# A mixture-of-experts stage that stores its results in token order with indirect scatters, and the stage behind it that reads them with plain loads

## The chip, the core and the metric

The kernel runs on one core of one Trainium2 chip. The metric is the device time of one execution in microseconds (us). The engines are TensorE (PE; its weight loads are listed apart as PEld), VectorE (DVE), ScalarE (ACT), GpSimd (POOL) and SyncE (SP), which issues DMAs. Each runs its own program in order, and they wait for each other on semaphores.

## The reference

16384 tokens (128 sequences of 128) of width 128, all in float32. Two layers, each with a retention and a feed-forward part; every part takes the normalised h and adds to it:

```python
h = tok_ref(x)                                   # three-tap embedding
h = h + attn0(layernorm(h))                      # retention, 8 heads
gate = softmax(xn @ gate_w + gate_b)             # xn = layernorm(h)
top_v, top_i = top_k(gate, 2); top_w = softmax(top_v)
for e in range(8):                               # experts, 128 -> 512 -> 128
    ce = sum(where(top_i == e, top_w, 0), -1)
    out += ce[..., None] * (relu(xn @ w1[e] + b1[e]) @ w2[e] + b2[e])
h = h + out
h = h + attn1(layernorm(h))                      # retention with complex weights
h = h + merged_ffn(layernorm(h))                 # weights mixed per sequence
```

The experts are computed sparsely: each token goes through its two experts only.

## The kernel before, in words

The program has four stages, one after the other: retention with routing (tiles `a_...`), experts (`b_...`), complex retention (`c_...`) and the merged feed-forward layer (`d_...`). h stays in SBUF (`h_all`). Stages a and c work in 32 groups of 4 sequences (GB = 4, 512 tokens). Each engine has one list of pieces for a step, written out by hand, in which piece k works on group n + k; the steps in the middle run in a loop, two groups in one turn, and the first and last ones are unrolled.

**Stage a.** POOL gathers embedding rows (4 indirect DMAs per group, L330). Later in the group, DVE finds each token's two experts (`choose`, L860 and L864) and its place in each expert's list (`place_tokens`, to `pos_cur`). POOL copies these places to `pos_all` (L339) and scatters the normalised rows `xn_mid` to the DRAM tensor `sent` in 8 indirect DMAs of 128 rows (L343), 4 of them at the end of one step and 4 at the beginning of the next. PE's products there begin with L399 (from the gathered rows) and L410 (the transposes of the normalised rows). At the end DVE works out the table of slots (L988 to L1042), and with it `moves`, by which a place in `sent` becomes a place in `done`.

**Stage b** goes through 78 slots: 57 of 512 rows and 21 of 256. A slot is a run of rows of one expert. The first 76 slots are 19 laps of three large and one small one (ROUND = 4), and 17 of the laps are a loop. SP loads the rows (`b_x`, L1155), the two weights (`b_w`, L1161 and L1164) and the bias (`b_b`, L1167), two slots ahead; the load of the fourth slot waits for fills with zeros, which POOL writes behind the lists (L1173 to L1180). PE multiplies (L1232, four banks), transposes the next slot's rows (L1223) and multiplies back (L1242). ACT and DVE take the ReLUs in turns (L1262, L1288). DVE adds the bias of the slot before (`y_keep`, L1296) and POOL stores it in the order of the slots with one plain DMA (L1208). In the first four slots POOL also turns `pos_all` into places in `done` (`move_places`, L1196 to L1204).

**Stage c.** POOL gathers each group's two result rows per token from `done` (8 indirect DMAs, L1462, two groups ahead), DVE adds them to h (L1805, L1812) and takes the statistics, ACT normalises, PE transposes (L1516) and goes through the products of a group: L1531 (queries), L1554 (states, small matmuls from `k_early`), L1570 (scores), L1591 and L1597 (values), L1609 (back to the tokens), L1620, L1630. DVE masks the scores (L1841) and the states (L1849), ACT copies the queries (L1709). POOL also makes `k_early` and `q_late` (L1473, L1480). SP has only the load of constants (L1440), and then of `tv` for stage d (L1443), which waits for the first group's h.

Of the kernel before, what the change touches and what calls it, by code (L numbers as in the profile page):

```python
# [7 lines left out]
ALU = mybir.AluOpType  # L8
# [10 lines left out]
GB = 4  # L19
# [11 lines left out]
PACK = B2 + D  # L31
# [9 lines left out]
SPARE_ROWS = SMALL_SPARE * TILE  # L41
SEQS = 16
# [77 lines left out]
def retention_phase(nc, h_all, w_all, pos_all, routing, sent_d, ids_d, table_d, wq_d, wqs_d, wkkv_d,  # L120
                    gn_w_d, gn_b_d, tabs_d, tabs_c_d, gate_w_d, gate_c_d, slot_c_d):
# [12 lines left out]
    with ExitStack() as ctx:  # L134
# [40 lines left out]
        slots, list_end, moves, _ = routing  # L175
# [13 lines left out]
        xn_mid = sb("xn_mid", [P, 2, GB, D])  # L189
# [33 lines left out]
        shifts = sb("shifts", [P, 2, E])  # L223
# [7 lines left out]
        ids_padded = sem("ids_padded")  # L231
# [53 lines left out]
        pos_kept = sem("pos_kept")  # L285
# [5 lines left out]
        LOADS = 11  # L291
# [7 lines left out]
        def _(sp):  # L299
# [11 lines left out]
            sp.dma_start(routing[3][:], tabs_c_d[:, 2 * P:3 * P]).then_inc(loaded, 16)  # L311

        @block.gpsimd
        def _(pool):
# [57 lines left out]
            pool.memset(ids[:, NB:], 0).then_inc(ids_padded, 1)  # L372
            pool.wait_ge(ids_loaded, 16)
            pool.wait_ge(ids_padded, 1)
# [4 lines left out]
            pool.wait_ge(pos_kept, NG)  # L379

        @block.tensor
        def _(pe):
# [128 lines left out]
            def turn_mid(s, g):  # L511
# [5 lines left out]
                for b in range(GB):  # L517
                    m = nc.tensor.transpose(work[1][:, b * T:(b + 1) * T], xn_mid[:, g.par, b, :], ident)
# [76 lines left out]
        def _(act):  # L595
# [33 lines left out]
            def mid_normalise(g):  # L629
# [4 lines left out]
                for b in range(GB):  # L634
                    m = nc.scalar.activation(xn_mid[:, g.par, b, :], h_all[:, bass.ds(g.n * GB + b, 1), :],
                                             ACT.Identity, scale=rstd_mid[:, b:b + 1], bias=shift_mid[:, b:b + 1])
# [93 lines left out]
        def _(dve):  # L730
# [125 lines left out]
            def choose(g):  # L856
# [5 lines left out]
                m.then_inc(chosen_step, 1)  # L862
                dve.wait_ge(chosen_step, g.n * 2 + 1)
# [17 lines left out]
            def place_tokens(g):  # L881
# [5 lines left out]
                if g.is_past(2):  # L887
                    dve.wait_ge(pos_kept, g.n - 1)
# [93 lines left out]
            def then(ins):  # L982
# [40 lines left out]
            base = region[:, 0, :]  # L1023
            also(v.tensor_copy(moves[:, 0, 0, :], base))
            also(v.scalar_tensor_tensor(out=moves[:, 1, 0, :], in0=used[:, 0:E], scalar=float(TILE), in1=base,
                                        op0=ALU.mult, op1=ALU.add))
            also(v.scalar_tensor_tensor(out=shifts[:, 0, :], in0=ends[:, 0:E], scalar=float(TILE), in1=base,
                                        op0=ALU.mult, op1=ALU.subtract))
            then(v.tensor_scalar(shifts[:, 1, :], reached[:, 0:E], float(SMALL), float(BIG * TILE), ALU.mult, ALU.add))
            then(v.tensor_tensor(shifts[:, 1, :], shifts[:, 1, :], moves[:, 1, 0, :], ALU.subtract))  # L1030
            also(v.tensor_tensor(moves[:, 1, 1, :], shifts[:, 1, :], shifts[:, 0, :], ALU.subtract))
            also(v.tensor_copy(moves[:, 0, 1, 0:1], shifts[:, 0, 0:1]))
            also(v.tensor_tensor(moves[:, 0, 1, 1:E], shifts[:, 0, 1:E], shifts[:, 1, 0:E - 1], ALU.subtract))
# [11 lines left out]
def experts_phase(nc, pos_all, routing, sent_d, done_d, pack_d):  # L1045


    slots, list_end, moves, ident = routing

    with ExitStack() as ctx:  # L1050
# [11 lines left out]
        zeros = sb("zeros", [P, J, D])  # L1062
        pos_f = sb("pos_f", [P, 2, NB, 2])
        moved = sb("moved", [P, NB, 2])
        x = sb("x", [P, 2, J, D])
        w = sb("w", [P, 2, B2])
        b2 = sb("b2", [P, 2, D])
# [4 lines left out]
        zeroed = sem("zeroed")  # L1072
# [1932 lines left out]
```

## Time and profile before

| | |
|---|---|
| time, median of 3 runs | 2535.09 us (2529.93 to 2538.09) |
| profiled execution: span | 2547.7 us; its own time is not given apart from the span |
| PE busy | 2127.2 us (83%) |
| DVE, ACT, POOL busy | 1437.5, 1346.8, 1044.3 us |
| DMA | 168.12 MB, mean 66 GB/s |
| mean granted clock of PE | 0.893 |

Views of the profile used here: the table of stretches gives busy time, number of instructions, granted clock (1.00 is 2.4 GHz, 0.50 is 1.2 GHz) and the share of the DMA engines' time. The list of waits says which engine and line stood idle, and what ended it: "issue" is idle time in which the engine waited for nothing that the profile shows, "remote" a releaser that it cannot name. The timeline merges equal instructions and puts idle time before them in brackets.

### The profile page before, as it was taken

How to read it: one execution, taken by the hardware profiler on the slowest of the kernel's cores; microseconds unless marked ns; L12 is line 12 of the kernel's file. 1: busy time of each engine (PE TensorE's matmuls, PEld its weight loads, DVE VectorE, ACT ScalarE, POOL GpSimd, SP SyncE). 2: the span in 40 equal slices, each digit the busy share in tenths (PEclk: the TensorE clock that was granted, in tenths of full speed). 3: DMA queues.
4: the chain of work that ended last, by engine and by line, in shares of the span. 5: the costliest groups of instructions: out<-in, count | busy, mean ns of one | idle time of the engine just before them, and what ended most of it. 6: DMA issues, size and time to landing. Idle time of an engine off the chain costs nothing. (4 is left out here: it accounts for less than half of the span.)

```text
span 2547.7 us, 56802 instructions
## 1 busy us (share of the span) xinstructions
PE 2127.2 (83%) x19420; PEld 1576.5 (62%) x19420; DVE 1437.5 (56%) x4270; ACT 1346.8 (53%) x2844; POOL 1044.3 (41%) x1133
## 2 busy tenths in 40 slices
PE   5888888888875999999994777777777779999998
PEld 2555555555554677777772455554455558999997
DVE  3766666666664222222323455554555567888877
ACT  3655555555552222222223555555555568999985
POOL 3556656656645600000005444444444402334444
PEclk8989989988985999999996788877888789999999
DMA  2111211211211555555551210000000001111111
GB/s 71 53 57 50 59 57 49 59 57 49 59 32 34 181 163 158 165 158 168 152 166 51 102 26 22 23 22 25 25 23 23 21 5 35 39 35 38 48 39 43
DMA packets 101867, 168.12 MB, mean 66 GB/s; under 512 B 19714, under 2 KB 50699, under 8 KB 101620
## 3 DMA queue, kind: packets, MB, share of 16 engines
q1 hardware_dynamic: 70900, 87.99, 12.1%
q0 software_dynamic: 30848, 78.56, 10.3%
q8 instruction: 73, 1.20, 0.2%
q14 instruction: 46, 0.38, 0.0%
HBM read 121.45 MB, written 45.02 MB: 65 GB/s over the span
## 5 line engine op out<-in xcount | busy, mean ns | idle before, releaser
L1288 DVE TENSOR_SCALAR b_hT<-b_hbank,b_w 128x512 f32<-128x512 f32 (+1 forms) x156 | 105.8, 678 | 369.8 <-PE b_hbank L1232 369.7
L343 POOL DMA_INDIRECT sent<-a_xn_mid,a_pos_cur x256 | 250.5, 979 | 73.4 <-issue 72.8
L1462 POOL DMA_INDIRECT c_rows<-done,c_cur_pos x256 | 244.3, 954 | 75.1 <-issue 74.7
L1262 ACT ACTIVATE b_hT<-b_hbank,b_w 128x512 f32<-128x512 f32 (+1 forms) x156 | 98.3, 630 | 322.7 <-PE b_hbank L1232 322.7
L1242 PE MATMUL b_bank<-b_w,b_hT 128*128 128x128 f32 x2160 | 254.2, 275 | 2.1 <-DVE b_hT L1288 2.1
L1242 PEld LDWEIGHTS b_bank<-b_w,b_hT 128*128 128x128 f32 x2160 | 247.5, 192 | 2.4 <-DVE b_hT L1288 2.3
L1232 PE MATMUL b_hbank<-b_xT,b_w 128*128 128x512 f32 (+1 forms) x624 | 247.1, 539 | 0.9 <-DMA b_w<-pack_dram 0.9
L1841 DVE TENSOR_TENSOR c_masked<-c_bank,c_decay 128x512 f32<-128x512 f32 x256 | 163.3, 681 | 138.3 <-remote 102.0
L1208 POOL DMA_DIRECT2D done<-b_y x78 | 42.3, 543 | 423.4 <-DVE b_y L1296 405.3
L450 PE MATMUL a_bank<-a_wkkv,a_xT 128*128 128x384 f32 x256 | 120.8, 557 | 106.3 <-issue 94.6
L744 DVE TENSOR_TENSOR a_masked<-a_scores,a_tabs 128x1024 f32<-128x1024 f32 x128 | 155.3, 1221 | 45.3 <-PE a_scores L474 25.3
L607 ACT ACTIVATE a_kv<-a_bank 128x384 f32<-128x384 f32 x128 | 62.4, 488 | 208.9 <-PE a_bank L450 112.9
L1232 PEld LDWEIGHTS b_hbank<-b_xT,b_w 128*128 128x128 f32 x624 | 113.4, 192 | 87.8 <-issue 83.2
L1473 POOL TENSOR_TENSOR c_k_early<-c_xn,c_k_decay 64x512 f32<-64x512 f32 x32 | 40.9, 1277 | 299.9 <-ACT c_xn L1683 299.8
L2536 ACT ACTIVATE d_wm<-d_bank 128x448 f32<-128x448 f32 (+1 forms) x160 | 147.3, 1095 | 26.0 <-PE d_bank L2262 25.6
L1591 PE MATMUL c_bank<-c_masked,c_vx 128*32 128x128 f32 x2048 | 119.8, 337 | 44.6 <-issue 43.2
L2715 DVE COPY d_wm<-d_bank 128x448 f32<-128x448 f32 (+1 forms) x160 | 144.5, 1055 | 21.3 <-PE d_bank L2262 21.3
L1554 PE MATMUL c_bank<-c_xn,c_k_early 64*32 64x32 f32 x1024 | 53.5, 204 | 118.6 <-issue 111.2
L2262 PE MATMUL d_bank<-d_g_diag,tv 64*128 64x112 f32 (+1 forms) x2368 | 144.7, 277 | 6.9 <-ACT d_wm L2536 5.1
L2262 PEld LDWEIGHTS d_bank<-d_g_diag,tv 64*128 64x128 f32 x2368 | 137.9, 190 | 13.0 <-ACT d_wm L2536 6.4
L450 PEld LDWEIGHTS a_bank<-a_wkkv,a_xT 128*128 128x128 f32 x256 | 41.4, 201 | 160.8 <-issue 160.5
L330 POOL DMA_INDIRECT a_rows<-table_dram,a_cur_ids x128 | 125.5, 980 | 34.6 <-issue 34.6
(256 smaller groups left out, 4925.9 us busy)
## 6 DMA issues: line engine op xcount, KB each, us to landing
b_w<-pack_dram SPq DMA_DIRECT2D x78, 258.0 KB, 2.7
b_w<-pack_dram SPq DMA_DIRECT2D x78, 256.0 KB, 2.7
b_x<-sent SPq DMA_DIRECT2D x57, 256.0 KB, 2.7
done<-b_y POOLq DMA_DIRECT2D x57, 256.0 KB, 2.4
d_b_all<-b_rows SPq DMA_DIRECT2D x32, 256.0 KB, 3.4
out_dram<-h_all SPq DMA_DIRECT2D x32, 256.0 KB, 2.3
b_b<-pack_dram SPq DMA_DIRECT2D x78, 64.0 KB, 1.9
tv<-tv_dram SPq DMA_DIRECT2D x1, 4736.0 KB, 15.7
```

Source lines behind the costliest of these rows:

```text
L330: pool.indirect_dma_start(out=rows[:, p, b, :], out_offset=None, in_=table_d, in_offset=bass.IndirectOffsetOnAxis(ap=cur_ids[:, p * GB + b ...
L343: pool.indirect_dma_start(out=sent_d, out_offset=bass.IndirectOffsetOnAxis(ap=pos_cur[:, g.par, b, k:k + 1], axis=0), in_=xn_mid[:, g.par, ...
L450: nc.tensor.matmul(work[K_BANK[b]][:, 0:3 * D], xT[:, g.par, b * T:(b + 1) * T], wkkv[:], start=True, stop=True).then_inc(k_full, 1)
L744: v.tensor_tensor(masked[:, p, 2 * i:2 * i + 2, :, :, :].rearrange("p r b a t -> p (r b a) t"), score_banks[i][:].rearrange("p r (x t) -> ...
L1232: nc.tensor.matmul(h_bank[c][:, 0:s.rows], w[:, s.par, c * P:(c + 1) * P], xT[:, 0:s.rows], start=True, stop=True).then_inc(h_full, 1)
L1242: m = nc.tensor.matmul(y_bank[s.par][:, j * D:(j + 1) * D], hT[:, c, j * P:(j + 1) * P], w[:, s.par, W2 + c * D:W2 + (c + 1) * D], start=( ...
L1462: pool.indirect_dma_start(out=rows[:, g.par, b, k, :], out_offset=None, in_=done_d, in_offset=bass.IndirectOffsetOnAxis(ap=cur_pos[:, g.pa ...
L1591: nc.tensor.matmul(to[rr, :, i, c * L:(c + 1) * L], vx[:, g.par, b, c, rr], masked[:, p, r, i, c, :, :], start=(i + c == 0), stop=False)
L1841: v.tensor_tensor(masked[:, p, r, :, :, :, :].rearrange("p i c k t -> p (i c k) t"), score_bank[r][:].rearrange("p (x t) -> p x t", t=L), ...
L2262: m = nc.tensor.matmul(banks[who][:, at:at + n], tv[half, blocks[j], :], g_diag[half, 0:cols[j], :], start=True, stop=True)
L2536: nc.scalar.activation(wm[:, :, half, at:at + n].rearrange("p s f -> p f s"), bank[:, 0:n * SEQS].rearrange("p (f s) -> p f s", s=SEQS), A ...
L2715: v.tensor_copy(wm[:, :, half, at:at + n].rearrange("p s f -> p f s"), bank[:, 0:n * SEQS].rearrange("p (f s) -> p f s", s=SEQS)).then_inc ...
```

## The change

Each row of `sent` becomes 130 numbers wide: the row, then the number of the token's first expert and a tag 2 x token + 8. DVE writes these two into `xn_mid` in `choose`. In stage b DVE makes the row of the result from them (`find_rows`: whether the slot's expert is not the token's first, plus the tag), and POOL scatters the slot's results with one indirect DMA per 128 rows, 4 for a large slot and 2 for a small one. `done` is thereby in token order, two rows per token, and SP loads a group's rows in stage c with one plain DMA. `pos_all`, `moves` and `move_places` go. The fills carry tags that lead behind the tokens. (The number of the expert stands in the pack's bias, whose load is one number wider.)

```diff
@@ retention_phase, POOL: scatter
                     pool.wait_ge(placed, g.n + 1)
-                    pool.tensor_copy(pos_all[:, bass.ds(g.n * GB, GB), :],
-                                     pos_cur[:, g.par, :, :]).then_inc(pos_kept, 1)
+                    pool.sem_inc(pool_step)
@@ retention_phase, DVE: choose
                 m.then_inc(chosen_step, 1)
+                v.tensor_tensor(xn_mid[:, g.par, :, D:WIDE], index[:, :, 0:2], tags[:, of_group(g), :], ALU.max)
                 dve.wait_ge(chosen_step, g.n * 2 + 1)
@@ retention_phase, DVE: place_tokens
                 if g.is_past(2):
-                    dve.wait_ge(pos_kept, g.n - 1)
                     dve.wait_ge(scattered[g.par], g.turn * (2 * GB * 16))
@@ retention_phase, DVE: end
-            base = region[:, 0, :]
-            also(v.tensor_copy(moves[:, 0, 0, :], base))
...
@@ experts_phase, SP: load
                 if s.is_past(2):
                     sp.wait_ge(x_turned, s.n - 1)
+                    sp.wait_ge(row_ready, s.n - 1)
                 sp.dma_start(x[:, p, 0:s.j, :], rows_of(sent_d, row, s)).then_inc(x_loaded[p], 16)
@@ experts_phase, POOL
-            pool.memset(zeros[:], 0.0).then_inc(zeroed, 1)
-            pool.wait_ge(zeroed, 1)
+            pool.memset(fill[:], 0.0).then_inc(fill_made, 1)
+            pool.dma_start(fill_tags[:], fill_tags_d).then_inc(fill_tagged, 16)
+            pool.wait_ge(fill_made, 1)
+            pool.wait_ge(fill_tagged, 16)
+            pool.tensor_copy(fill[:, :, D + 1], fill_tags[:]).then_inc(fill_made, 1)
...
             def store(prev, s, nxt):
+                pool.wait_ge(row_ready, s.n + 1)
                 pool.wait_ge(y_ready, s.n + 1)
-                pool.dma_start(rows_of(done_d, s.out_row, s), y[:, s.par, 0:s.j, :]).then_inc(stored[s.par], 16)
-                if isinstance(s.n, int) and s.n < ROUND:
-                    move_places(s.n)
+                for j in range(s.j):
+                    if j == 0:
+                        pool.sem_inc(spaced)
+                    pool.indirect_dma_start(
+                        out=done_d, out_offset=bass.IndirectOffsetOnAxis(ap=row[:, s.k, j:j + 1], axis=0),
+                        in_=y[:, s.par, j, :], in_offset=None).then_inc(stored[s.par], 16)
@@ experts_phase, DVE
+            def find_rows(s):
+
+                dve.wait_ge(x_loaded[s.par], s.turn * 16 + 16)
+                dve.wait_ge(b2_loaded[s.par], s.turn * 16 + 16)
+                if s.is_past(ROUND):
+                    dve.wait_ge(stored[s.par], s.stores_far * 16)
+                v.scalar_tensor_tensor(out=row[:, s.k, 0:s.j], in0=x[:, s.par, 0:s.j, D], scalar=b2[:, s.par, D:D + 1],
+                                          in1=x[:, s.par, 0:s.j, D + 1], op0=ALU.not_equal,
+                                          op1=ALU.add).then_inc(row_ready, 1)
...
                 relu(s, 3)
                 if is_last(s):
                     y_keep(s)
+                else:
+                    find_rows(nxt)
@@ complex_retention_phase, SP
-            sp.wait_ge(h_done, 1)
-            sp.dma_start(tv[:], tv_d).then_inc(tv_loaded, 16)
+            def load_rows(g):
+
+                if g.is_past(2):
+                    sp.wait_ge(h_ready, g.n - 1)
+                sp.dma_start(
+                    rows[:, g.par, :, :, :].rearrange("t b k d -> t b (k d)"),
+                    done_d[bass.ds(g.n * (2 * GT) + E, 2 * GT), :].rearrange("(b t k) d -> t b (k d)", t=T, k=2),
+                ).then_inc(rows_loaded[g.par], 16)
+
+            def step(s):
+                if g := s.at(0):
+                    load_rows(g)
+                    if s.is_edge() and s.n == C_LOOP + 1:
+                        sp.wait_ge(h_done, 1)
+                        sp.dma_start(tv[:], tv_d).then_inc(tv_loaded, 16)
@@ complex_retention_phase, POOL
-            def take_pos(g):
...
-            def gather(g):
...
-                        pool.indirect_dma_start(
-                            out=rows[:, g.par, b, k, :], out_offset=None, in_=done_d,
-                            in_offset=bass.IndirectOffsetOnAxis(ap=cur_pos[:, g.par, b, k:k + 1], axis=0),
-                        ).then_inc(gathered[g.par], 16)
```

## Rows read from the trace of the kernel before

**Rows 1.** Stretches by stage: length, busy us and instructions of PE, PEld, DVE, ACT, POOL; clock, DMA share, GB/s

```profile
0.00:826.00 826.00, 643.06 (x4292) 414.27 (x4292) 532.71 (x1806) 431.69 (x871) 466.65 (x518) 0.88 0.18 53
826.00:1343.00 517.00, 506.56 (x3054) 386.92 (x3054) 145.42 (x234) 140.38 (x234) 81.75 (x126) 0.99 0.55 162
1343.00:2082.00 739.00, 538.49 (x7368) 367.43 (x7368) 387.71 (x1042) 387.49 (x706) 330.92 (x353) 0.80 0.11 31
```

**Rows 2.** List of waits, 1400 to 2000 us: total us, times, longest

```profile
...
ACT c_q L1709 <- remote: 107.7, 25, 7.1
PE c_bank L1554 <- issue: 100.5, 134, 1.9
...
```

**Rows 3.** Timeline of one group of stage c: start, us, engine, line, what, count, idle before

```profile
1607.42 1.01 POOL L1462 DMA_INDIRECT c_rows<-done,c_cur_pos  x1 [0.16 <-issue]
...
1608.32 1.17 PE L1570 MATMUL c_bank<-c_q,c_x_heads 32*128 32x128 f32 x32
...
1610.48 0.32 PE L1554 MATMUL c_bank<-c_xn,c_k_early 64*32 64x32 f32 x14
...
1613.17 0.30 PE L1554 MATMUL c_bank<-c_xn,c_k_early 64*32 64x32 f32 x5 [1.18 <-issue]
...
1614.63 0.35 PE L1554 MATMUL c_bank<-c_xn,c_k_early 64*32 64x32 f32 x4 [1.16 <-issue]
1614.75 0.69 DVE L1841 TENSOR_TENSOR c_masked<-c_bank,c_decay 128x512 f32<-128x512 f32 x1 [4.82 <-remote]
...
1616.23 0.94 POOL L1462 DMA_INDIRECT c_rows<-done,c_cur_pos  x1 [0.30 <-issue]
```

**Rows 4.** Stretches of one group each in stage c, columns as in rows 1

```profile
1605.50:1627.50 22.00, 15.89 (x233) 11.05 (x231) 11.88 (x34) 11.85 (x23) 9.75 (x12) 0.84 0.09 24
2035.10:2047.90 12.80, 12.67 (x233) 9.18 (x231) 11.77 (x34) 11.78 (x23) 1.48 (x2) 1.00 0.01 1
```

**Rows 5.** Timeline of PE: L1609 of the first group

```profile
1401.59 2.04 PE L1609 MATMUL c_bank<-c_wv,c_z 128*128 128x128 f32 x16
```

**Rows 6.** Timeline of PE in stage a, before and after the first scatter at 94.12 us

```profile
72.13 0.63 PE L410 MATMUL a_bank<-a_tabs_c,a_xn 128*128 128x128 f32 x4 [1.01 <-ACT a_kv L607]
...
75.35 1.13 PE L399 MATMUL a_bank<-a_rows,a_tabs_c 128*128 128x512 f32 x2
...
93.58 1.12 PE L399 MATMUL a_bank<-a_rows,a_tabs_c 128*128 128x512 f32 x2
...
501.82 1.13 PE L399 MATMUL a_bank<-a_rows,a_tabs_c 128*128 128x512 f32 x2
...
525.56 1.12 PE L399 MATMUL a_bank<-a_rows,a_tabs_c 128*128 128x512 f32 x2
```

**Rows 7.** Timeline of the second slot of stage b

```profile
841.83 3.60 PE L1232 MATMUL b_hbank<-b_xT,b_w 128*128 128x512 f32 x8
...
842.89 0.69 ACT L1262 ACTIVATE b_hT<-b_hbank,b_w 128x512 f32<-128x512 f32 x1 [3.84 <-PE b_hbank L1232]
...
845.70 3.74 PE L1242 MATMUL b_bank<-b_w,b_hT 128*128 128x128 f32 x32
...
849.27 3.60 PE L1232 MATMUL b_hbank<-b_xT,b_w 128*128 128x512 f32 x8
```

**Rows 8.** Timeline of the start of stage c

```profile
1347.30 0.43 SPq L1440 DMA_DIRECT2D c_blocks<-c_blocks_dram  x1
...
1355.47 1.14 DVE L1805 SCALAR_TENSOR_TENSOR c_first_in<-c_rows,w_all,h_all 128x128 f32<-128x128 f32 x4 [4.14 <-DMA c_rows<-done,c_cur_pos]
```

**Rows 9.** Page, DMA issues: count, KB each, median us from issue to landing

```profile
d_b_all<-b_rows SPq DMA_DIRECT2D x32, 256.0 KB, 3.4
```

**Rows 10.** Timeline: three operations that the change's new or removed ones resemble

```profile
525.38 0.19 POOL L339 COPY pos_all<-a_pos_cur 128x8 uint32 x1
...
798.49 0.29 DVE L860 TENSOR_TENSOR a_one_hot<-a_gate_c,a_index 128x32 f32<-128x32 f32 x2
...
826.48 0.53 POOL L1173 MEMSET b_zeros<- 128x512 f32 x1 [1.73 <-POOLq L134]
```

More of the change, by code:

```diff
@@ L1060, in experts_phase @@
         h_bank = [ctx.enter_context(nc.psum_tensor(f"b_hbank{i}", [P, 512], F32)) for i in range(C)]
[L1062 to L1065, printed above, removed]
+        fill = sb("fill", [P, FILL_BLOCKS, WIDE])
+        fill_tags = sb("fill_tags", [P, FILL_BLOCKS])
+        x = sb("x", [P, 2, J, WIDE])
+        row = sb("row", [P, ROUND, J], U32)
         w = sb("w", [P, 2, B2])
-        b2 = sb("b2", [P, 2, D])
+        b2 = sb("b2", [P, 2, D + 1])
         xT = sb("xT", [P, TILE])
@@ L1103, in __init__, with count_blocks @@
                 self.entry = lap + (more + BIG) if small else lap * (ROUND - 1) + before
-                self.out_row = (lap * SMALL + (BIG * TILE + more * SMALL) if small else
-                                lap * ((ROUND - 1) * TILE) + before * TILE)
-        class LastSlot(Group):
+                self.count_blocks(lap, more)
+            def count_blocks(self, lap, more):
+                of_round = 2 * J if self.k % 2 == 0 else J + SMALL // P
+                self.blocks = lap * ROUND_BLOCKS + (more * ROUND_BLOCKS + self.k * J)
+                self.stores = lap * of_round + (more * of_round + self.k // 2 * J)
+                self.stores_far = self.stores - (of_round - (SMALL // P if self.k == ROUND - 1 else J))
+        class LastSlot(Slot):
             def __init__(self, n):
@@ L1183, in _ @@
-            steps = 0
-            def then(ins):
-                nonlocal steps
-                steps += 1
-                ins.then_inc(place_step, 1)
-                pool.wait_ge(place_step, steps)
-            def move_places(part):
-                if part == 0:
-                    then(pool.tensor_copy(pos_f[:, 0, :, :], pos_all[:]))
-                    then(pool.tensor_copy(pos_f[:, 1, :, :], pos_f[:, 0, :, :]))
-                for i in range(part * 4, part * 4 + 4):
-                    e, kind = divmod(i, 2)
-                    then(pool.tensor_scalar(moved[:], pos_f[:, 0, :, :], moves[:, kind, 0, e:e + 1],
-                                            moves[:, kind, 1, e:e + 1], ALU.is_ge, ALU.mult))
-                    then(pool.tensor_tensor(pos_f[:, 1, :, :], pos_f[:, 1, :, :], moved[:], ALU.add))
-                if part == 3:
-                    then(pool.tensor_copy(pos_all[:], pos_f[:, 1, :, :]))
+                               .rearrange("(p j) d -> p j d", j=J),
@@ L1305, in step @@
                     y_keep(s)
+                else:
+                    find_rows(nxt)
+            find_rows(slot_at(0, 0, 0))
             run_slots(dve, step)
```

118 lines of the change are left out of this document (54 added, 64 removed).

## The prediction, as put on record

> **What bounds the kernel now.** I first cut the span into its four stages [rows 1]: retention a (to 826 us), experts b (to 1343), complex retention c (to 2082) and the merged layer d. TensorE (PE) is the busiest engine in each, but by how much differs. In b it works 507 of 517 us at a granted clock of 0.99: that stage is PE's. In c it is busy for 538 of 739 us at 0.80, so something keeps it waiting.
>
> The waits of c come next [rows 2]. PE's largest idle time is in front of L1554 and is called "issue": it waits for nobody that the view can name. ACT waits as long for a "remote" releaser in front of L1709, which takes what PE makes. The timeline of one group shows why [rows 3]. At 1607.42 POOL begins eight indirect gathers and ends them at 1617.17. PE writes down its small matmuls until 1610.8 and from then on only a few every 1.4 us. The mask at 1614.75 needs scores that PE had written down by 1609.5: DVE waited 4.82 us for them. So while a run of indirect DMAs is under way, what PE finishes is told to others late, and then PE itself halts.
>
> The same stage has its own control: from 2035 us on, behind the last gathers, it goes on working. Both stretches hold a whole group [rows 4]: 233 matmuls, 34 DVE and 23 ACT instructions in each. The first lasts 22.0 us with 12 POOL instructions at clock 0.84, the second 12.8 us with 2 of them at 1.00. Stage a agrees [rows 6]: its groups are 18.2 us apart before the scatters of L343 start, and 23.7 us with them.
>
> Here a page speaks against this reading. The Trainium skill, "SBUF — State Buffer", section "Who interferes with whom", says that DMA never contends with a compute engine and that PE and ACT wait on no one. By that rule the 9.2 us between the two groups would have another cause, and the sum would have next to nothing in stage c. The trace differs (22.0 against 12.8 us), so I go by the rows; what the rule would make of the time is a rival below.
>
> **The change, part by part.**
> Stage c, removed: 256 gathers (8 per group) and the index copies of L1451. In their place SP issues one plain 512 KB load per group, up to two groups ahead. The nearest row is a 256 KB load in four blocks, 3.4 us to landing [rows 9]; twice that is 7 us and lies under a group of 13. Now 28 periods run from the first L1609 [rows 5] to the one with which the second stretch begins [rows 4]: (2035.1 - 1401.6)/28 = 22.6 us. The new period cannot be far below 12.8, where PE is busy for 12.67 of 12.80 us [rows 4]; ACT (11.8) and DVE (11.8) are next. I take 13.2, since the loop's groups need an address computed that the last ones have as constants: 28 x (22.6 - 13.2) = **263 us less**. Bounds of this term: 274 (12.8) and 227 (14.5).
> The head of c: the first combine waited 4.14 us for its gathers [rows 8]; SP has the plain load behind ten small loads, issued by 1347.7, so it lands about when DVE is ready. The next three groups fill the pipeline each behind a gather run of 10 us. I take 4 + 10 = **14 us less**, between 4 and 25. The load of tv (L1443) now stands behind the eighth row load on SP; the row loads are two groups ahead, which covers it.
>
> Stage b, added: 57 x 4 + 21 x 2 = 270 indirect scatters for 78 plain stores, one every 1.26 us as in [rows 3], so 5.0 us of POOL in a slot of 7.4 [rows 7]: POOL fits. The question is what they do to PE. The trace bounds it from both sides. Nothing: a run of four is short, and what it delays has room: the first ReLU of a slot ends 1.75 us after the slot's start and is wanted at 3.9 [rows 7]. Most: c loses (22.0 - 12.8)/8 = 1.15 us per indirect DMA. Between them a's runs of eight cost (23.7 - 18.2)/8 = 0.69 us each, and a's runs of four left a wait of 1.01 us in PE behind them [rows 6], 0.25 each. Nearest is the run of four, and b has 2.1 us of room where a had none: I take 0.04 each, **10 us more**, and keep 0 and 186 (270 x 0.69) for the range.
> DVE gains find_rows, one operation on 128x4 per slot, under 0.2 us as each of the two of L860 [rows 10]; it stands behind the slot's last ReLU, where DVE waits for PE. It waits for the bias load, which SP issues when y is kept; that lands some 2 us later, 3 us before DVE's next ReLU, and nobody else stands behind it on DVE. SP's new wait on it for the load of x comes two slots ahead: nothing. If that cover went, PE would wait for a ReLU.
> POOL loses move_places (32 passes in the first four slots); they delay the first stores, and I give back 2 us. The last store becomes two scatters: 2 us more. The fill tile grows from 512 to 4160 elements, 0.53 us to about 4.3 [rows 10]; the fills are wanted only by the fourth slot's load: nothing, at most 3.
> Stage a: a DVE operation of about 0.2 us per group (half of L860's pair is 0.15), 6 us over 31 groups if it is on the path; POOL's copy of L339, 0.19 us [rows 10] and a gap about as long, goes from in front of each scatter run, 9 us if that is on the path. **3 us less**, between +6 and -9. Scatter rows of 520 instead of 512 bytes: DMA is at a share of 0.18 there [rows 1], nothing.
>
> Sum: -263 - 14 + 10 - 3 = **-270 us**. The profiled execution has a span of 2547.7 us, 0.5% over the median of 2535.09; its own time is not given apart from that. The difference goes against the median: 2535 - 270 = **2265 us**.
>
> **Rivals.**
> *The scatters hold PE in b as they do in a* (0.69 each): +186 instead of +10, 2441 us. For it: b issues its small L1242 matmuls (32 in 3.74 us [rows 7]) just while a run is under way. Against: four in a row, not eight, and L1232 is slow in issue. 15%.
> *Stage c finds another bound*, at the 18 us that stage a has with runs of four: 28 x 4.6 = 129 instead of 263, 2399 us. For it: ACT is busy 11.8 of 12.8 us and any late semaphore would show. Against: the group of 12.8 us had the same DVE and ACT work. 13%.
> *The gathers were hidden*: c's long groups come from something else in the loop, as the page's rule has it. Then c gives 4 us of its head and b costs its 2: about 2535, no change. For it: the views name no releaser. Against: the halts begin and end with the runs, and a's period grows when the scatters begin. 4%.
> *Slower*: every scatter in b costs c's price, 270 x 1.15 = 310 us, and PE's halts let the granted clock fall from 0.99 to c's 0.84, another 517 x (0.99/0.84 - 1) = 92. With the other terms' -280 that is 122 more, 2657 us. It decides from 1.04 us per scatter on, in PE's wait in front of L1242. For it: b is the one stage with no slack on PE. Against: a's runs of four. 4%.
>
> **How the numbers follow.** The forecast has 64%, its own range 2240 to 2310. The 80% range reaches down to 2225 (all terms at their better bound) and up to 2430, which takes in the second rival and the lower part of the first. About 0.3% is what a measurement of this kernel can tell from no change. Faster by more: 64 + 15 + 13 = 92%; within it 4%; slower 4%.
>
> **What would show it.** In the changed kernel's stage c, the line that is L1609 here comes every 13 to 14 us, "issue" in front of L1554 and the "remote" waits are gone, and the granted clock is near 1. In b, L1242 and L1232 keep their idle time near zero and slots stay at 7.4 us; a slot of 9 to 10 us and idle in front of L1242 or L1223 is the first rival. In a, groups stay near 23.7 us. The prediction is wrong if c keeps its 22 us, or if b grows by more than 60 us.

## The result and the profile after

The changed kernel takes 2285.12 us (median of 4 runs, 2282.15 to 2288.43), the kernel before on the same chip 2536.59 us (4 runs): a ratio of 0.9007, with a 95% interval of 0.8988 to 0.9027. That is 251.5 us less; 2265 was forecast, with 2225 to 2430 as the range. The two profiled executions are further apart: spans of 2547.7 and 2280.5 us, 267.2 us. The profiled execution of before was longer than each of its four timed runs (2529.93 to 2542.56 us). The sum of the terms was -270.

The same cut into stages as in [rows 1], of the changed kernel. Columns as there.

```profile
0.00:826.00 826.00, 642.16 (x4293) 415.00 (x4294) 532.29 (x1830) 432.11 (x871) 464.02 (x488) 0.88 0.18 54
826.00:1361.00 535.00, 513.77 (x3039) 387.40 (x3040) 159.97 (x310) 135.12 (x234) 261.63 (x280) 0.99 0.54 156
1361.00:1816.00 455.00, 421.51 (x7384) 304.32 (x7384) 394.30 (x1033) 381.09 (x707) 84.13 (x68) 0.96 0.15 51
1816.00:2280.50 464.50, 435.64 (x4706) 406.59 (x4706) 372.62 (x1201) 386.16 (x1033) 164.98 (x137) 0.97 0.14 39
```

Stage c is 284 us shorter, at a granted clock of 0.96 in place of 0.80. Stage b is 18 us longer at the same 0.99; POOL works 262 us in it in place of 82. Stages a and d are as they were.

One group of the changed c, as in [rows 4] (first fence); and its largest waits from 1409 to 1771 us, as in [rows 2] (second fence).

```profile
1602.90:1615.80 12.90, 12.77 (x232) 9.27 (x230) 12.11 (x33) 11.79 (x23) 2.60 (x3) 1.00 0.12 41
```

```profile
POOL c_k_early L1482 <- ACT c_xn L1689: 303.9, 29, 11.6
PEld c_bank L1576 <- issue: 22.1, 29, 0.9
PEld c_bank L1560 <- issue: 21.2, 28, 0.8
```

Every group of the loop is now like the single group that the kernel before had behind its last gathers: 12.9 us, PE busy for 12.77 of them, clock 1.00. The 100 us of "issue" in front of PE's small matmuls of L1554 and the 108 us of "remote" in front of ACT are gone. The one large wait that is left is POOL's own.

The trace also holds the time of each update of a semaphore, and this tells what "remote" was. In the group of [rows 3], PE's last score matmuls (L1570) end at 1609.47 to 1609.49 us, and the updates that they send stand at 1613.19 to 1614.67; the mask of DVE, which waits for them, starts at 1614.75. Between 1420 and 2030 us of the kernel before, 147 of 485 updates by PE stand more than 0.5 us behind the end of their matmul (a lost record counts as late in this); behind the last gathers it is none of 48, and in the changed c none of 485.

To place the 267 us more closely than by stage, the timeline of PE at four places: the first and the last slot of b, the first group of c and the one 28 periods on. The kernel before first, then the changed one.

```profile
832.23 2.08 PE L1232 MATMUL b_hbank<-b_xT,b_w 128*128 128x512 f32 x2 [0.92 <-DMA b_w<-pack_dram]
...
1336.23 1.46 PE L1232 MATMUL b_hbank<-b_xT,b_w 128*128 128x256 f32 x6
...
2035.12 1.95 PE L1609 MATMUL c_bank<-c_wv,c_z 128*128 128x128 f32 x16
```

```profile
827.74 2.07 PE L1219 MATMUL b_hbank<-b_xT,b_w 128*128 128x512 f32 x2 [0.79 <-DMA b_w<-pack_dram]
...
1356.70 1.46 PE L1219 MATMUL b_hbank<-b_xT,b_w 128*128 128x256 f32 x6
...
1408.82 2.04 PE L1615 MATMUL c_bank<-c_wv,c_z 128*128 128x128 f32 x16
...
1771.31 2.04 PE L1615 MATMUL c_bank<-c_wv,c_z 128*128 128x128 f32 x16
```

With 1401.59 from [rows 5] the stretches are:

| stretch | before, us | after, us | difference | forecast |
|---|---|---|---|---|
| start to b's first slot | 832.2 | 827.7 | -4.5 | -3 |
| b, first to last slot | 504.0 | 529.0 | +25.0 | +8 |
| end of b to c's first group | 65.4 | 52.1 | -13.3 | -12 |
| 28 periods of c | 633.5 | 362.5 | -271.0 | -263 |
| the rest | 512.6 | 509.2 | -3.4 | 0 |

(b's forecast is the 10 us of the scatters less the 2 of move_places; the third row's is the head of c, -14, and the two last scatters, +2.)

The one row of the table that came out at another size is b. Its full slots did not change; its small ones did. Here is the changed kernel from a full slot into a small one and the next: PE and ACT first (lines L1219 and L1229 are the up and down matmuls, L1249 ACT's ReLU), then POOL and find_rows.

```profile
1012.00 3.60 PE L1219 MATMUL b_hbank<-b_xT,b_w 128*128 128x512 f32 x8
1015.65 3.74 PE L1229 MATMUL b_bank<-b_w,b_hT 128*128 128x128 f32 x32
1019.22 1.89 PE L1219 MATMUL b_hbank<-b_xT,b_w 128*128 128x256 f32 x8
...
1022.79 2.05 PE L1229 MATMUL b_bank<-b_w,b_hT 128*128 128x128 f32 x16 [1.23 <-ACT b_hT L1249]
...
1014.39 1.27 ACT L1249 ACTIVATE b_hT<-b_hbank,b_w 128x512 f32<-128x512 f32 x2 [5.08 <-PE b_hbank L1219]
...
1022.26 0.84 ACT L1249 ACTIVATE b_hT<-b_hbank,b_w 128x256 f32<-128x256 f32 x2 [5.95 <-PE b_hbank L1219]
...
1016.56 0.96 POOL L1195 DMA_INDIRECT done<-b_y,b_row  x1 [3.21 <-issue]
...
1020.35 0.96 POOL L1195 DMA_INDIRECT done<-b_y,b_row  x1 [0.30 <-issue]
...
1017.92 0.22 DVE L1292 SCALAR_TENSOR_TENSOR b_row<-b_x,b_b 128x2 uint32<-128x2 f32 x1 [1.51 <-issue]
```

And the same small slot of the kernel before:

```profile
989.50 1.89 PE L1232 MATMUL b_hbank<-b_xT,b_w 128*128 128x256 f32 x8
...
991.67 1.50 PE L1242 MATMUL b_bank<-b_w,b_hT 128*128 128x128 f32 x12
...
990.14 0.47 ACT L1262 ACTIVATE b_hT<-b_hbank,b_w 128x256 f32<-128x256 f32 x1 [3.54 <-PE b_hbank L1232]
```

Before, a small slot's first ReLU starts 0.64 us after its first matmul. Now the four scatters of the slot two back run from 1016.56 to 1021.31, and the first ReLU starts at 1022.26, 3.04 us after the first matmul. PE had ended the matmuls for the four ReLUs at 1019.82 to 1021.12; their updates stand at 1022.24 to 1022.37. The down matmuls stand 3.57 us behind the slot's start in place of 2.17. In 8 of the 17 small slots of the rounds in the middle the first ReLU starts at 1.6 us already, but the later ones are as late as here, so that each of them takes 5.1 to 5.5 us in place of 4.0. In the full slot ahead of it the first ReLU is late as well (2.39 us after 1012.00), and there it costs nothing. The round of four slots grew from 26.1 us to between 27.2 and 27.7. find_rows takes 0.22 us, and nobody waits for it.

### The profile page after: what moved, and what is told of

It reads as the page before. It is cut to its first block and busy times, and to the rows that moved or that the text cites. A ratio compares the mean times of both kernels' runs of the same rounds, so it can differ in the third digit from the quotient of the medians.

```text
span 2280.5 us, 56952 instructions
## 1 busy us (share of the span) xinstructions
PE 2013.1 (88%) x19420; PEld 1513.3 (66%) x19420; DVE 1459.2 (64%) x4372; ACT 1334.5 (59%) x2844; POOL 974.8 (43%) x972
## 5 line engine op out<-in xcount | busy, mean ns | idle before, releaser
L1195 POOL DMA_INDIRECT done<-b_y,b_row x270 | 258.5, 957 | 266.7 <-issue 266.4
L1249 ACT ACTIVATE b_hT<-b_hbank,b_w 128x512 f32<-128x512 f32 (+1 forms) x156 | 95.3, 628 | 364.5 <-PE b_hbank L1219 345.0
L1229 PE MATMUL b_bank<-b_w,b_hT 128*128 128x128 f32 x2160 | 259.8, 277 | 18.4 <-ACT b_hT L1249 12.4
L1229 PEld LDWEIGHTS b_bank<-b_w,b_hT 128*128 128x128 f32 x2160 | 249.2, 192 | 23.7 <-ACT b_hT L1249 12.4
L1219 PE MATMUL b_hbank<-b_xT,b_w 128*128 128x512 f32 (+1 forms) x624 | 248.5, 541 | 2.8 <-issue 2.0
L1219 PEld LDWEIGHTS b_hbank<-b_xT,b_w 128*128 128x128 f32 x624 | 113.5, 192 | 91.5 <-issue 87.0
L2293 PE MATMUL d_bank<-d_wm,d_hT 128*128 128x128 f32 x1024 | 135.3, 277 | 0.3
L2277 PE MATMUL d_bank<-d_xT,d_wm 128*128 128x128 f32 x1024 | 135.4, 277 | 0.0
L2277 PEld LDWEIGHTS d_bank<-d_xT,d_wm 128*128 128x128 f32 x1024 | 124.7, 192 | 8.4 <-issue 6.7
```

The lines of the kernel that those rows point to most:

```text
L1195: pool.indirect_dma_start(out=done_d, out_offset=bass.IndirectOffsetOnAxis(ap=row[:, s.k, j:j + 1], axis=0), in_=y[:, s.par, j, :], in_off ...
L1219: nc.tensor.matmul(h_bank[c][:, 0:s.rows], w[:, s.par, c * P:(c + 1) * P], xT[:, 0:s.rows], start=True, stop=True).then_inc(h_full, 1)
L1229: m = nc.tensor.matmul(y_bank[s.par][:, j * D:(j + 1) * D], hT[:, c, j * P:(j + 1) * P], w[:, s.par, W2 + c * D:W2 + (c + 1) * D], start=( ...
L2277: m = nc.tensor.matmul(banks[who][:, j * T:(j + 1) * T], wm[:, s, 0, c * P:(c + 1) * P], xT[:, q.par, s, :], start=True, stop=True)
L2293: m = nc.tensor.matmul(bank[:, (s % GB) * D:(s % GB + 1) * D], hT[:, s % AHEAD, c, :], wm[:, s, 1, c * D:(c + 1) * D], start=(c == 0), sto ...
```

## The experiments

Twelve kernels ran, in four sets, each set on one chip beside the kernel before. In the first three of them the kernel before had medians from 2546.72 to 2548.71 us, near the 2536.59 of the result above. The last set is different and is told at the end.

**c alone.** In the kernel before:

```
-  for b, k: pool.indirect_dma_start(rows[:, g.par, b, k, :], in_=done_d, ... cur_pos[:, g.par, b, k:k + 1])
+  sp.dma_start(rows[:, g.par, :, :, :], done_d[g.n * (2 * GT) : + 2 * GT])     # one per group
```

> The kernel before with stage c's part of the change alone: the eight indirect gathers of a group become one plain 512 KB load by SP (its rows are those that lie at the group's place, not its tokens' own, so the output is not the reference's), and b keeps its plain stores. Theory (the gathers of POOL hold PE): c's groups come every 12.95 us as in the changed kernel, b stays at 26.0 us per round of four slots, and the time is 2536 - 271 - 13 = about 2252 us, 25 to 33 us below the changed kernel's 2285. Rival 1 (the gain belongs to the two parts together, as rows that b scattered to token order are read better): c's groups stay above 13.5 us, 2270 us or more. Rival 2 (something else in c's loop sets its 22.6 us): about 2536.

Measured: 2256.43 us (before 2548.29; ratio 0.8854, 0.8832 to 0.8877). Its c has 28 periods of 12.96 us, and its rounds of b take 26.1 us. So the gain is the gathers' removal alone, and what stage b's scatters pay for it is the 25 us of the table. Rivals 1 and 2 are out.

**b's scatters away, the rest of the change kept.**

```
-  for j in range(s.j): pool.indirect_dma_start(done_d, ... row[:, s.k, j:j + 1], in_=y[:, s.par, j, :])
+  pool.dma_start(done_d[s.blocks * P : + s.rows], y[:, s.par, 0:s.j, :])
```

> The changed kernel with one plain store by POOL per slot in b in place of the four or two indirect scatters; find_rows, its waits and SP's wait on it stay (rows land in the order of the slots, so stage c reads other tokens' results). Theory (the scatters make PE's semaphore updates late, and only the slot of 256 rows has no room for it): the small slots go back from 5.3 to 4.0 us, a round from 27.3 to 26.0, and the time is 2285 - 25 = 2260 us. Rival (find_rows on DVE, or SP's new wait, is what lengthens the small slot): a round stays at 27.3 us and the time at 2285.

Measured: 2267.06 us (ratio 0.8887, 0.8856 to 0.8918), rounds of 26.1 us with small slots of 4.0. So it is the scatters, not find_rows or SP's wait. From its first to its last slot b takes 501.8 us here, 2.2 below the kernel before, which had move_places in it, and 27.2 below the changed kernel: that is the price of the 270 scatters, 0.10 us each. The total is 7 us above the expectation, and the profile says where: stage a, which is the changed kernel's own, ended later.

```profile
847.19 2.04 PE L1215 MATMUL b_hbank<-b_xT,b_w 128*128 128x512 f32 x2 [0.78 <-DMA b_w<-pack_dram]
```

b begins at 847.2 us here and at 827.7 in the profile of the result. In the three further kernels with the changed stage a untouched or nearly so it begins at 844.5, 847.1 and 849.7; in five profiles with the stage a of before, at 828.9 to 832.8. The forecast's term for a (-3, between -9 and +6) held in the pair above. On this set's chip, where both stages a ran, b begins 14 to 18 us later with the changed one (847.2 against 828.9 to 832.8), outside the term's bounds; over all these profiles it is 12 to 21. In the four profiles the groups of a come every 24.5 to 24.7 us, in place of 24.0 in the pair. What makes the difference stays open; the later runs are therefore read by stage.

**Which scatters.** Two kernels take away those of one slot in four: of k = 1, two ahead of the small slot, and of k = 2, just ahead of it.

```
+  if s.k == 1 and s.j == J:        # the second kernel: s.k == 2
+      pool.dma_start(aside_d[s.blocks * P : + s.rows], y[:, s.par, 0:s.j, :]); return
```

> The changed kernel with the results of one slot in four, the one two ahead of the small slot (k = 1), stored plainly by POOL to a tensor aside, the other slots' scatters as they are (stage c reads 512 KB of the experts' weights in place of done, so that it reads nothing unwritten; the output is not the reference's). Theory (the run of four that POOL begins in slot k = 2 reaches into the small slot, whose first ReLU has no room to be late): the small slots fall from 5.3 to 4.0 us, a round to 26.0, the time to 2285 - 25 = 2260 us. Rival (each scatter has its small price, wherever it stands): taking 77 of 270 away gives back 77/270 of 25, 7 us: 2278, small slots at about 5.

> As the run before, but for the slot just ahead of the small one (k = 2), whose scatters are issued in the slot of 512 rows behind the small one. As many scatters are taken away, 76 of 270. Theory: nothing changes, small slots stay at 5.3 us, a round at 27.3, 2285 us (at most 4 less). Rival (a price for each scatter): 2278 us, as for the other slot.

Measured: 2298.97 us (ratio 0.9028, 0.9010 to 0.9046) and 2304.96 us (ratio 0.9051, 0.9033 to 0.9069), both beside 2546.72. The comparison by stage is with a kernel of the same set whose stage b is the changed kernel's (the first one under "Semaphore instructions in between"): its b takes 534.1 us from the first to the last slot. Without the scatters of k = 2 it is 533.6, with small slots at 5.6 and a round at 27.7 us: 76 scatters fewer gave back nothing, as expected. Without those of k = 1 it is 521.3: the small slots are back at 4.0 us, and yet a round takes 27.2. PE and ACT of that kernel:

```profile
1037.85 1.89 PE L1224 MATMUL b_hbank<-b_xT,b_w 128*128 128x256 f32 x8
1041.80 3.60 PE L1224 MATMUL b_hbank<-b_xT,b_w 128*128 128x512 f32 x8
1049.42 0.47 PE L1234 MATMUL b_bank<-b_w,b_hT 128*128 128x128 f32 x2 [0.24 <-issue]
1050.25 1.12 PE L1224 MATMUL b_hbank<-b_xT,b_w 128*128 128x512 f32 x2 [0.35 <-ACT b_xT L1261]
...
1049.52 0.60 ACT L1261 ACTIVATE b_xT<-b_bank 128x512 f32<-128x512 f32 x1 [4.26 <-remote]
```

The slot behind the small one (from 1041.80) takes 8.5 us. The scatters of k = 2 and of the small slot are six in a row, from 1040.79 to 1048.10, and ACT's copy of x waits 4.26 us for PE's word that it has turned the rows (PE ended that at 1045.83, and the update stands at 1049.42). Its releaser is "remote", as ACT's was in the c of before. The length of the run alone is not it. The changed kernel has the same six in a row in every round (1024.48 to 1031.75 in the round shown above); they begin 0.2 to 0.5 us ahead of the slot of 512 rows, which then takes 7.4 to 7.6 us, while here they begin 1.0 us ahead of it. My theory had the place right and the end wrong: 25 us was to come back, and 13 did. The rival's 7 is missed too, and for k = 2 the rival fails altogether (0.5 in place of 7). Neither a price per scatter nor one tight place describes b; where a run falls in the slots decides.

**Holding two of them back.** The changed kernel, with

```
   for j in range(s.j):
+      if j == 2 and s.k == 1:
+          pool.wait_ge(h_act, s.n * 2 + 5); pool.sem_inc(spaced)
```

> The changed kernel, all work in it, with the last two of the four scatters of slot k = 1 held by POOL until ACT has made the first ReLU of the small slot. The run that reaches into the small slot is then two long and ends before it starts. Theory: small slots at 4.0 to 4.3 us, a round at 26.0 to 26.5, 2285 - 20 = about 2265 us. Rival (the lateness only moves on: the two held scatters stand with the next four in one run of six, and the slot behind the small one waits): a round stays at 27.3 us or more, 2285 to 2300.

Measured: 2329.87 us (ratio 0.9147, 0.9123 to 0.9170), worse than the changed kernel. The rival was right, and by more than it said: rounds take 28 to 30 us.

```profile
1016.15 1.89 PE L1222 MATMUL b_hbank<-b_xT,b_w 128*128 128x256 f32 x8
1016.79 0.47 ACT L1252 ACTIVATE b_hT<-b_hbank,b_w 128x256 f32<-128x256 f32 x1 [3.54 <-PE b_hbank L1222]
...
1018.07 0.96 POOL L1198 DMA_INDIRECT done<-b_y,b_row  x1 [2.27 <-ACT b_hT L1252]
...
1023.86 0.69 ACT L1252 ACTIVATE b_hT<-b_hbank,b_w 128x512 f32<-128x512 f32 x1 [4.66 <-PE b_hbank L1222]
...
1024.39 0.96 POOL L1198 DMA_INDIRECT done<-b_y,b_row  x1 [0.30 <-issue]
...
1026.82 2.94 PE L1232 MATMUL b_bank<-b_w,b_hT 128*128 128x128 f32 x24 [1.06 <-DVE b_hT L1278]
```

The small slot is as of old (its first ReLU 0.64 us after its first matmul), but six scatters then run from 1018.07 to 1025.35, and the next slot's first ReLU comes 3.76 us after its first matmul at 1020.10.

**What about the DMAs is it?** Two kernels changed the gathers in the c of before. One put work of POOL between them, leaving nothing out:

```
   pool.indirect_dma_start(rows[:, g.par, b, k, :], ...)
+  pool.wait_ge(pos_ready, <number of those before>)
+  pool.tensor_tensor(filler[:, 1, :], filler[:, 0, :], filler[:, 0, :], ALU.add)     # 128 x 256
```

> The kernel before with an addition of 256 numbers per partition (about 0.65 us of POOL) behind each of stage c's eight gathers, nothing left out. The same gathers are issued, but no two stand back to back: eight take 15 us of POOL in place of 10, of a period of 22.6. Theory A (it is the run that hurts: PE's updates pile up while POOL issues without a break, and drain in the gaps): c's groups fall to 16 to 19 us, 2536 - 28 x 5 = about 2400 us. Theory B (each indirect DMA costs PE about 1.15 us, wherever it stands): groups stay within 1 us of 22.6, 2536 us or up to 30 more.

Measured: 2398.06 us (ratio 0.9407, 0.9376 to 0.9438). This is theory A's figure to 2 us, and theory B is out: eight gathers per group are there, 256 additions have come on top, and 150 us are gone. (Each addition comes with a wait for the ones before it, so POOL pauses and computes; no kernel here had the pause alone.) Periods are 17.2 us, which is about POOL's own turn (8 x 1.77 us and 2.8 us of its other work).

```profile
1602.21 1.01 POOL L1463 DMA_INDIRECT c_rows<-done,c_cur_pos  x1 [0.16 <-issue]
1603.24 0.64 POOL L1469 TENSOR_TENSOR c_filler<-c_filler 128x256 f32<-128x256 f32 x1
1604.03 0.96 POOL L1463 DMA_INDIRECT c_rows<-done,c_cur_pos  x1 [0.16 <-issue]
```

The other made them plain DMAs of the same size, still from POOL:

```
-  pool.indirect_dma_start(rows[:, g.par, b, k, :], in_=done_d, ... cur_pos[...])
+  pool.dma_start(rows[:, g.par, b, k, :], done_d[g.n * (2 * GT) + (b * 2 + k) * T : + T])
```

> The kernel before with each of stage c's eight indirect gathers made a plain DMA of 128 rows (64 KB), still issued by POOL (the rows are those at the group's place, so the output is not the reference's). Theory A (any DMA whose descriptors POOL writes holds PE while it is written, the plain one for 0.54 us as b's store shows): runs of eight take some 7 us and cost about half, groups of 16 to 19 us, about 2400 us. Theory B (only indirect DMAs do it): groups of 13 us, 2536 - 28 x 9.6 - 10 = about 2257 us.

Measured: 2261.70 us (ratio 0.8872, 0.8843 to 0.8901), periods of 12.97 us. Theory B: eight DMAs of 64 KB back to back from POOL cost PE nothing when they are plain (12.97 us against 12.96 with none from POOL), and none of 474 updates by PE in this c is late. From the timeline of POOL:

```profile
1607.08 4.28 POOL L1462 DMA_DIRECT2D c_rows<-done  x8
```

POOL is at each for 0.54 us, where the indirect ones take 0.96.

**Semaphore instructions in between.** A cheaper spacing was tried in stage a of the changed kernel, then in the c of before:

```
   pool.indirect_dma_start(...)
+  for _ in range(4): pool.sem_inc(pool_step)      # in c: pos_ready
```

> The changed kernel with four semaphore increments by POOL (nobody waits for them) behind every indirect DMA of stage a, so that none starts 1.26 us behind the last; no other edit. Spacing brought stage c's groups of the kernel before from 22.6 to 17.2 us. Theory A (back-to-back indirect DMAs hold PE in a as well, and a short break lets it catch up): if the four take 0.2 to 0.5 us, a's groups fall from 23.9 to 19 to 21 us, 2285 - 31 x 4 = about 2160 us. Theory B (a's groups are bound by another chain since the scatters wait for the routing): groups stay at 23.9 us or grow by the added POOL time, 2285 to 2330 us.

> The kernel before with four semaphore increments by POOL behind each of stage c's eight gathers. The run on stage a showed that POOL makes them while it is at the DMA, which still come every 1.27 us, and that a's groups grew from 23.9 to 27.2 us, 3.3 us for 48 of them. Theory A (semaphore instructions of POOL join what waits while an indirect DMA is issued, and make it worse): c's 32 per group add 32/48 x 3.3 = about 2 us to 22.6, 2536 + 28 x 2.2 = about 2600 us. Theory B (a's growth was of a's own, through POOL's turn): c's groups stay within 0.5 us of 22.6.

Measured: 2405.24 us for a (ratio 0.9453, 0.9437 to 0.9469) and 2565.03 us for c (ratio 1.0061, 1.0041 to 1.0081, beside 2548.71). The increments make no break: the DMAs still come every 1.25 to 1.3 us, with the same 0.30 of "issue" between them.

```profile
512.77 1.01 POOL L347 DMA_INDIRECT sent<-a_xn_mid,a_pos_cur  x1 [0.31 <-issue]
514.08 0.97 POOL L347 DMA_INDIRECT sent<-a_xn_mid,a_pos_cur  x1 [0.30 <-issue]
```

In a they cost a great deal all the same. Groups come every 27.5 us, where the three other profiles of this chip, with the changed a as it is, have 24.5 to 24.6, and b begins at 937.9 us in place of 844.5 to 849.7. Neither theory had that. In c they cost 0.4 us a period (23.04 against 22.63), within theory B's half a microsecond, and far from the 2 us of theory A. Stage a has 48 increments in a group and c has 32; why a pays some seven times as much is open.

**The same spacing in stages a and b of the changed kernel.** All of the kernel's work is in it; behind each of its 654 indirect DMAs (384 in a, 270 in b) POOL waits for what came before and adds two rows of 128 numbers per partition.

```
   pool.indirect_dma_start(...)
+  pool.wait_ge(spaced, s.n + (s.blocks + (j + 1)))          # in a: ids_ready, pool_step
+  pool.tensor_tensor(filler[:], fill[:, 0, 0:128], fill[:, 0, 0:128], ALU.add).then_inc(spaced, 1)
```

> The changed kernel, all work in it, with an addition of 128 numbers per partition by POOL (half of that in the run on c, so about 0.32 us) behind each indirect DMA of stages a and b. They then come every 1.45 us in place of 1.27. Theory A (a break in which POOL computes lets PE's updates through): a's groups fall from 23.9 to 20.5 to 22 us, b's small slots from 5.4 to 4.0 to 4.6 us, so 2285 - 31 x 2.5 - 15 = about 2190 us. Theory B (what helped c was only its period's slack, and in a POOL's longer turn, 12 x 0.2 = 2.3 us, is added to the group): a's groups 24 to 26 us, 2300 to 2360 us.

> As the run before with additions of 32 numbers per partition (about 0.1 us), so that the indirect DMAs come every 1.3 us or so. Theory A says how much of a break is needed: if any break in which POOL is not at a DMA does, a's groups fall as much as or more than with 128 numbers, to about 2180 us; if the break's length counts, the gain is about a quarter of that, 2260 us. Theory B: 2285 to 2310 us.

Measured: 2216.20 us with 128 numbers (ratio 0.8690, 0.8672 to 0.8708) and 2233.20 with 32 (ratio 0.8759, 0.8739 to 0.8779), both beside 2548.71. The intervals lie below that of the changed kernel (0.8988 to 0.9027, beside the kernel before on the result's chip; it did not run on this one). As far as ratios from two chips can be compared, this version beats both. Theory A holds in kind (2190 was its figure), and the gain of 3% on the changed kernel comes with additions whose results nobody reads. With 128 numbers, from a full slot of b into a small one:

```profile
985.26 0.42 POOL L1207 TENSOR_TENSOR b_filler<-b_fill 128x128 f32<-128x128 f32 x1
...
990.11 1.89 PE L1230 MATMUL b_hbank<-b_xT,b_w 128*128 128x256 f32 x8
990.13 0.97 POOL L1203 DMA_INDIRECT done<-b_y,b_row  x1 [0.17 <-issue]
...
990.75 0.47 ACT L1260 ACTIVATE b_hT<-b_hbank,b_w 128x256 f32<-128x256 f32 x1 [3.54 <-PE b_hbank L1230]
991.13 0.41 POOL L1207 TENSOR_TENSOR b_filler<-b_fill 128x128 f32<-128x128 f32 x1
...
991.71 0.98 POOL L1203 DMA_INDIRECT done<-b_y,b_row  x1 [0.17 <-issue]
...
992.28 1.95 PE L1240 MATMUL b_bank<-b_w,b_hT 128*128 128x128 f32 x16
...
993.30 0.98 POOL L1203 DMA_INDIRECT done<-b_y,b_row  x1 [0.17 <-issue]
```

The scatters run through the whole small slot, one every 1.58 us, and its first ReLU still starts 0.64 us after its first matmul, as in the kernel before. Rounds are at 26.1 us: the 25 us of b are back with all 270 scatters in place. In a, groups come every 22.5 us in place of 24.0, where 20.5 to 22 were expected; it is what POOL needs for twelve DMAs at 1.58 and its two sums. From 300 to 680 us:

```profile
300.00:680.00 380.00, 323.83 (x2297) 194.12 (x2294) 303.54 (x953) 227.41 (x462) 339.92 (x458) 0.94 0.19 59
```

POOL is busy for 340 of 380 us: a has another bound now. With 32 numbers (a DMA every 1.42 us) b's rounds are at 27.1 us, so a break of 0.25 us is too short there; in a the mean is 22.4, with nine of 26 groups at 21.3 to 21.5 and three at 26 to 27.4. The total lies between the two figures that theory A had for it (2180 and 2260).

**A length between, and the chip on which nothing was to be gained.** 64 numbers in a, 128 in b.

> The changed kernel, all work in it, with additions of 64 numbers in stage a and of 128 in b behind each indirect DMA. With 128 numbers (0.41 us, a DMA every 1.58 us) b's rounds went to 26.1 us and a's groups to 22.4, which is POOL's own turn there: 12 x 1.58 + 2 x 1.26 + small = about 22 us. With 32 (0.26 us, every 1.42 us) a's groups were mostly 21.3 us but now and then 26, and b's rounds stayed at 27.1. Theory A (0.3 us of break is enough in a, and POOL is then the bound): a's groups at 21.0 to 21.5 us, b's rounds at 26.1, 2216 - 31 x 1.1 = about 2185 us. Theory B (what is short of 0.4 us lets single groups stall, as with 32): a's groups at 22 to 22.6 us in the mean, 2205 to 2225 us.

Measured: 2188.47 us, near theory A's 2185, with b's rounds at 26.1; a's groups come every 21.8 us, between the two theories. But the kernel before, beside it on this set's chip, took 2118.10 us (9 runs, 2114.57 to 2123.61) at a granted clock of 0.964 to 0.972, where it had 2547 to 2549 us and 0.89 to 0.90 in the three other sets and 2537 us beside the result. The ratio is 1.0326 (1.0308 to 1.0345): here the spaced version is slower than the kernel before. So the 2188 can't be held against the 2216 of another chip, and whether 64 numbers are better than 128 is not decided.

This kernel's own trace is from that chip, and it shows what differs. POOL is at an indirect DMA for 0.98 us, as with 128 numbers on the other chip, and the parts without halts take as long as elsewhere: b 502.2 us (502.6 there with the same breaks), 28 periods of c 362.6 (362.5 in the changed kernel), the rest 509.3 (509.2). But between 200 and 640 us, in stage a, none of 480 updates by PE is late. With the longer break of 128 numbers on the other chip 59 of 479 are, with 32 numbers 170 of 479, and 144 of 504 in the changed kernel's a. Its a is busy with POOL, as the stretch from 300 to 650 us shows (305 of 350 us), so it also says nothing on how short a break may be.

```profile
300.00:650.00 350.00, 300.51 (x2143) 181.08 (x2142) 285.61 (x894) 210.75 (x429) 305.32 (x431) 0.95 0.20 60
```

One more thing differs. The records of updates by DMAs are nearly complete here (17440 of 17840), while the trace of the changed kernel holds 7967 of 17840. So where updates are late, records are lost as well. All times here are of recorded executions, and whether the recording has a part in the halts is not shown.

How can the kernel before be 430 us faster? Its own trace on this chip is not there, but its trace of [rows 1] says what the halts of PE cost. The last L399 of its stage a:

```profile
717.90 1.13 PE L399 MATMUL a_bank<-a_rows,a_tabs_c 128*128 128x512 f32 x2
```

From 93.58 [rows 6] to there are 26 groups, 24.0 us each; at the 18.2 us of the groups ahead of the scatters they would be 151 us shorter. Stage c without halts is 271 us shorter in its periods and 13 in its head, by the table above. As an estimate, 2547.7 - 151 - 271 - 13 = 2113 us; the spans on this chip were 2112.7 to 2121.9. It fits a chip on which runs of indirect DMAs do not hold PE at all, which is also what the updates above say. The changed kernel did not run there. By the same reckoning (2280.5, less 150 for its a without halts and 25 for b's rounds at 26.1) it would come to about 2105, the same within 0.4%. That is an estimate, not a result.

## Why the prediction was right, and where it was not

*The sum.* The terms said -270, and the two profiles are 267.2 apart. Some of that is luck: b came out 17 us worse than forecast, and c's periods (8), its head (1), a (1.5) and the rest (3.4) together 14 us better. The forecast of 2265 us is 20 below the 2285 measured for another reason than the terms. It took a difference between profiles off a median, and the profiled execution of before was about 13 us above the median of its kernel (a run's time is 1.7 us over its span in the other runs), while that of the changed kernel was 3 us below its own.

*That the gathers hold PE in c, and not something else of the loop.* Right where the result and the first three sets ran: c alone gives 2256 us, and the same eight DMAs made plain give 2262. *28 periods of 13.2 us.* The bound from the kernel's own last groups (12.8) was the better value: 12.95, 271 us in place of 263. The addition for the computed address was not needed. *The head of c*: 13.3 in place of 12, and by two terms that were both too small. Where b's stores are plain and c's gathers gone, the stretch is 47.6 us in place of 65.4: the head gives 17.8 (14 was taken), and the last two scatters cost 4.5 (2 was taken).

*b, 0.04 us per scatter, "a run of four is short, and what it delays has room".* This is the step that failed in size: 25 us in place of 8, or 27 in place of 10 for the scatters by themselves. The room was read from a full slot alone [rows 7]. There it is true; the first ReLU is 1.3 us later and nothing moves. The small slot's down matmuls begin 2.2 us after its start, and its ReLUs are now so late that this costs 1.1 to 1.5 us in each of the 17 small slots in the middle. One row more in the reading, the small slot's, would have shown that it has less room. The first rival, which feared 0.69 us for each of the 270, is out at 0.10 in the mean. "Four in a row, not eight" was the reason against it, and that was a misreading of the change: the scatters of the slot ahead of the small one and the small slot's two stand six in a row in every round. They cost little where they fall, by the timing and not by their number, and the kernel that held two scatters back (rounds of 28 to 30 us) shows how near the rival is.

*a, -3 between -9 and +6.* -4.5 in the pair, but 12 to 21 later in four other profiles, 14 to 18 on one and the same chip. The term does not hold there. I had costed the edits as durations on a path; that a stage hangs on when POOL's runs meet PE's work, and so doesn't add up like that, is my reading and not shown. About 1 us of the 4.5 has a source that the prediction didn't name: DVE no longer computes the moves at the end of a. 2.9 us are there before that, when DVE copies the counts of the lists (811.94 against 809.02), and have no known source.

*"The gathers were hidden", 4%.* It follows from the Trainium skill, "SBUF — State Buffer", section "Who interferes with whom", by which DMA contends with no compute engine. The runs of the result and of three sets speak against it as a rule on time (22.0 against 12.8 us for the same group, with PE's updates and not the data late); whether SBUF has a part in that, no run shows. The last set's 2118 us is about what the kernel would take if the rule held, by the estimate above (2113). The 4% was for a mistake in my reading; that another chip could behave otherwise I hadn't considered, and it was the larger risk.

*The slower rival* needed 1.04 us per scatter; b's granted clock stayed at 0.99.

## What to carry to other kernels

When POOL issues indirect DMAs back to back, look at what PE's semaphores do meanwhile: a consumer waiting for "remote" or a PE row long done, and PE itself idle on "issue" behind it. Make such transfers plain where the order of rows allows. Where it doesn't, a break in which POOL computes helped here; that POOL's real work, put between them rather than around them, does the same was not tried. The costs are not additive, so read the tightest place of each kind of slot, not the most frequent one, and run the kernel on more than one chip before a version is chosen for this reason.

## What the runs showed of the hardware that was not expected

- During runs of indirect DMAs from POOL, one every 1.26 us, PE's semaphore updates came late (up to 5.2 us in the group of [rows 3]) and PE halted; with plain DMAs from POOL, eight back to back at 0.54 us each, neither happened (12.97 us per group against 22.6).
- A break of 0.41 us of POOL's computing behind each removed the cost in b (round 26.1), one of 0.25 us did not (27.1), and four semaphore increments behind each made no break at all and cost 3 us per group in stage a, 0.4 in c.
- The kernel before had medians of 2537 to 2549 us beside the result and in three sets on three chips, and of 2118 on the last set's. On that chip indirect DMAs with breaks of 0.30 us left none of 480 updates by PE late. Why it differs, and what it is between POOL and PE that holds the updates, stays open: no run here separates the writing of the descriptors from the reading of the row numbers.
